# Linear attention in chunks of 64 tokens instead of 128, with all score masks on VectorE

## The reference

```python
q, k = relu(q) + 1e-6, relu(k) + 1e-6
kv = cumsum(einsum('bhld,bhle->bhlde', k, v), axis=2)
num = einsum('bhld,bhlde->bhle', q, kv)
den = maximum(einsum('bhld,bhld->bhl', q, cumsum(k, axis=2)), 1e-6)
out = (num / den) @ out_w.T + out_b
```

## Time and profile before

| | |
|---|---|
| Median of 3 runs | 380.64 us (379.93 to 380.88) |
| Span of the profiled execution | 377.9 us |
| Around the span (median less span) | 2.7 us |
| TensorE busy | 356.6 us, 94% of the span |
| VectorE busy | 296.1 us, 78% |
| GpSimd busy | 279.1 us, 74% |
| ScalarE busy | 162.6 us, 43% |

### The profile page before, as it was taken

One profiled execution on the slowest core, in us unless ns is written; L12 is line 12 of the kernel. 1 busy time (PEld: TensorE's weight loads), 2 busy tenths in 40 slices (PEclk: granted clock), 3 DMA queues, 4 the chain that ended last, 5 costly groups with the idle time before them and its releaser, 6 DMA issues. The chain is left out here.

```text
span 377.9 us, 10670 instructions
## 1 busy us (share of the span) xinstructions
PE 356.6 (94%) x3514; PEld 255.6 (68%) x3514; DVE 296.1 (78%) x922; ACT 162.6 (43%) x394; POOL 279.1 (74%) x414
## 2 busy tenths in 40 slices
PE   8999999999999999999999999999899989998781
PEld 4566677777677777767777777778676556655451
DVE  2588788898989898888898878886756588799462
ACT  2463553454455346436436524442456435331120
POOL 5338987766777866877867789898978888578455
PEclk9999999999999999999999999999999999999897
DMA  8993881200300120032121013003000233148750
GB/s 255 328 308 88 251 245 22 66 16 16 72 31 16 35 53 16 19 83 87 55 49 39 25 25 67 16 20 80 16 31 28 73 97 111 57 146 283 220 181 23
DMA packets 39309, 34.50 MB, mean 91 GB/s; under 512 B 4505, under 2 KB 38456, under 8 KB 39256
## 3 DMA queue, kind: packets, MB, share of 16 engines
q1 hardware_dynamic: 36392, 29.54, 27.7%
q0 software_dynamic: 1312, 3.37, 2.9%
q10 hardware_dynamic: 1552, 0.92, 0.9%
HBM read 17.55 MB, written 12.60 MB: 80 GB/s over the span
## 5 line engine op out<-in xcount | busy, mean ns | idle before, releaser
L1650 POOL TENSOR_TENSOR s_t<-s_t,causal 128x512 f32<-128x512 f32 x63 | 78.9, 1273 | 15.6 <-ACT s_t L961 15.4
L539 PE MATMUL bank<-h1t,w_qkv 128*128 128x512 f32 x112 | 52.9, 595 | 0.4 <-DVE x L1220 0.3
L1207 DVE TENSOR_TENSOR s_t<-sbank,causal 128x512 f32<-128x512 f32 x65 | 43.5, 671 | 1.1 <-PE sbank L560 1.0
L1642 POOL TENSOR_TENSOR state_wide<-state,own_pair 128x256 f32<-128x256 f32 x28 | 18.9, 676 | 25.5 <-DVE state L1198 24.4
L961 ACT ACTIVATE s_t<-sbank 128x512 f32<-128x512 f32 x63 | 33.7, 587 | 7.8 <-PE sbank L560 7.8
L560 PE MATMUL sbank<-arena 32*128 32x256 f32 x512 | 36.7, 400 | 0.0
L599 PE MATMUL bank<-s_t,vp 128*32 128x128 f32 x1024 | 34.6, 275 | 1.1 <-DVE s_t L1207 0.4
L546 PE MATMUL bank<-w_qkv,h1t 128*128 128x256 f32 x128 | 34.2, 389 | 0.0
L1658 POOL TENSOR_TENSOR rr<-ve,neg_half 128x3 f32<-128x3 f32 x36 | 31.9, 887 | 3.0
L684 PE MATMUL bank<-w_out,attn_t 128*128 128x256 f32 x128 | 33.6, 385 | 0.5 <-DVE attn_t L1288 0.5
L778 PE MATMUL sbank<-h1t,w 128*128 128x512 f32 x72 | 33.0, 596 | 0.5 <-ACT h1t L961 0.5
(11 more groups left out here) (231 smaller groups left out, 831.5 us busy)
## 6 DMA issues: line engine op xcount, KB each, us to landing
rden_t<-rden SPq DMA_DIRECT2D x64, 64.0 KB
rows<-x SPq DMA_DIRECT2D x32, 128.0 KB, 1.7
x<-in_x SPq DMA_DIRECT2D x7, 512.0 KB, 8.6
out<-x SPq DMA_DIRECT2D x7, 512.0 KB
we<-in_we SPq DMA_DIRECT2D x1, 2048.0 KB
xmask<-in_mask POOLq DMA_DIRECT2D x2, 616.0 KB, 10.3
rows<-empty SPq DMA_DIRECT2D x1, 1032.0 KB, 5.2
we<-in_we SPq DMA_DIRECT2D x1, 1024.0 KB
```

Source lines behind the costliest of these rows:

```text
L539: mm = pe.matmul(dst[:, :], w_qkv[:, ch, cb * P:(cb + 1) * P], h1t[:, g % 3, ch, :], start=(ch == 0), stop=(ch == CH - 1))
L1207: dve.tensor_tensor(s_t[:, r, :, :], sbank[r][:, :].rearrange("p (s q) -> p s q", s=4), causal[:, :].unsqueeze(1).to_broadcast([P, 4, P]), ...
L1650: pool.tensor_tensor(s_t[:, r, :, :], s_t[:, r, :, :], causal[:, :].unsqueeze(1).to_broadcast([P, 4, P]), ALU.mult)\
```

## The change

Scores, masks and numerators are formed in chunks of 64 tokens. The two chunks of a tile lie side by side in the partitions: chunk c has its keys in partitions 64c to 64c+63. Scores of a tile take half the columns. The state is now advanced twice per tile, `inner_state` (between the two chunks) and `next_state`, each a 128x64 sum from PSUM; the parity factor moves into `own_block`, by which GpSimd multiplies (512 elements per partition instead of 256). Numerators move from bank 3 into free columns of score banks 2 and 3, so that `scores` of a tile now waits for `attn_t` and both state sums. Score tiles `s_t` are double. All four banks of scores are masked by VectorE in two instructions (512 elements each, two banks at a time), both at the start of its step. ScalarE's copies and GpSimd's masks go. The numbers of small matmuls change: `scores` 8 to 16 per tile, `numerators` 16 to 32, `from_state` 2 to 16, `key_values` 8 to 16.

The core of the diff:

```diff
 def scores(t):
-    wait(pe, s_masked, 2 * t)
-    wait(pe, s_copied, 2 * t)
+    wait(pe, s_masked, on_dve(t))
+    wait(pe, attn_ready, t)
+    wait(pe, state_ready, states(t + 1))
...
+            for c in range(2):
+                for r in range(RG):
+                    both = sbank[r][chunk(c), 2 * ch * CK:2 * (ch + 1) * CK].rearrange("p (s n) -> p s n", s=2)
+                    mm = pe.matmul(both, kt(slot, ch)[rows, part(t, c)], qpair(slot, ch)[rows, :, part(t, c)],
+                                   start=True, stop=True)
...
 def numerators(t):
+                v_of = vp[chunk(c), t % 3, head // 2, 32 * par:32 * par + 32]
+                mm = pe.matmul(sbank[2 + c][32 * r:32 * r + 32, at:at + CK], v_of,
+                               s_t[chunk(c), t % 2, r, 2 * ch + par, :],
...
+def inner_state(t):
+    wait(dve, st_done, t + 1)
...
+        dve.tensor_tensor(now, sums_of(0), state[:, t % 3, 0, :, :].rearrange("p c e -> p (c e)"), ALU.add)\
+            .then_inc(state_ready, 1)
+def next_state(t):
+    wait(dve, state_ready, states(t) + 1)
...
+def mask_scores(t, r):
+    dve.tensor_tensor(s_t[:, t % 2, r:r + 2, :, :],
+                      sall[:, r:r + 2, 0:4 * CK].rearrange("p r (a n) -> p r a n", a=4),
+                      causal_ck[:, :].unsqueeze(1).unsqueeze(1).to_broadcast([P, 2, 4, CK]), ALU.mult)\
+        .then_inc(s_masked, 1)
...
 def step(pool, i):
+    wait(pool, state_ready, states(M) + 1)
+    wait(pool, num_done, M - 1)
+    pool.tensor_tensor(state_wide[:, M % 2, c:2, :, :, :].rearrange("p k c r e -> p (k c) r e"),
...
-    for r in range(on_act(M + 1) - on_act(M)):
-        wait(pool, s_copied, 2 * M + r + 1)
```

More of the change, by code:

```diff
@@ L349, in tok, with part, chunk @@
             return slice((t % GT) * P, (t % GT + 1) * P)
+        def part(t, c):
+            first = (t % GT) * P + c * CK
+            return slice(first, first + CK)
+        def chunk(c):
+            return slice(c * CK, (c + 1) * CK)
         def starts(t):
@@ L578, in from_state @@
                 slot = (t // GT) % 2
-                wait(pe, h1t_ready, min(t + 1 + AHEAD + 1, NT))
-                wait(pe, x2_ready, t - 2)
-                wait(pe, wide_ready, updates(t))
-                for ch in range(CH):
-                    pe.matmul(bank[3][:, ch * P:(ch + 1) * P],
-                              state_wide[:, (t - 1) % 2, ch, :, :].rearrange("p r e -> p (r e)"),
-                              qall(slot, ch)[:, tok(t)], start=(ch == 0), stop=False, skip_group_check=True)
+                wait(pe, s_copied, on_act(t + 1))
+                wait(pe, s_masked, on_dve(t + 1))
+                wait(pe, wide_ready, t + 1)
+                for c in range(1 if starts(t) else 0, 2):
+                    for ch in range(CH):
+                        for r in range(RG):
+                            at = D + ch * CK
+                            pe.matmul(sbank[2 + c][32 * r:32 * r + 32, at:at + CK], state_wide[:, t % 2, c, ch, r, :],
+                                      qall(slot, ch)[:, part(t, c)], start=(ch == 0), stop=False, skip_group_check=True)
             def numerators(t):
-                wait(pe, h1t_ready, min(t + 1 + AHEAD + 1, NT))
-                wait(pe, x2_ready, t - 2)
                 first = starts(t)
@@ L637, in step @@
                     mm.then_inc(sc_done, 1)
-                if is_tile(V):
-                    wait(pe, ktok_ready, K + 1)
-                    values(V)
-                if i > NT:
-                    gate_products(pe, i - NT - 1, 1)
-                if is_tile(M) and not starts(M):
-                    from_state(M)
                 if i == NT - 1:
@@ L651, in step @@
                 if is_tile(M):
+                    from_state(M)
                     numerators(M)
[L653 to L667 removed]
                 if i == 0:
@@ L670, in step @@
                     pe.wait_ge(prep_dve, 5)
+                if is_tile(K):
+                    key_values(K)
+                if i > NT:
+                    gate_products(pe, i - NT - 1, 1)
+                if is_tile(F):
+                    wait(pe, x2_ready, i - 3)
+                    tr_h1(F, bank[3])
+                if is_tile(V):
+                    wait(pe, ktok_ready, K + 1)
+                    values(V)
+                if is_tile(K) and K % GT == 0:
+                    denominators(K // GT)
                 if is_tile(K):
@@ L1184, in by_queries @@
                 dve.tensor_tensor(qkc(g % 2, ch), ksum(g % 2, ch), qall(g % 2, ch), ALU.mult).then_inc(qkc_ready, 1)
-            def new_state(t):
-                u = updates(t)
-                wait(dve, st_done, u + 1)
-                wait(dve, wide_ready, updates(t - 2))
-                wait(dve, state_ready, 2 * u)
-                added = bank[3][:, D:D + CH * 2 * HD].rearrange("p (c s e) -> p c s e", c=CH, s=2)
-                for par in range(2):
-                    own = parity[:, par:par + 1]
-                    now = state[:, t % 3, :, par, :]
-                    if starts(t):
-                        dve.tensor_scalar(now, added[:, :, par, :], own, None, ALU.mult).then_inc(state_ready, 1)
-                    else:
-                        dve.scalar_tensor_tensor(out=now, in0=added[:, :, par, :], scalar=own,
-                                                 in1=state[:, (t - 1) % 3, :, par, :], op0=ALU.mult, op1=ALU.add)\
-                            .then_inc(state_ready, 1)
@@ L1202, in mask_scores @@
-            def mask_scores(t, lo=0, hi=RG):
-                own = range(on_act(t + 1) - on_act(t), RG)
-                for r in own[lo:hi]:
-                    wait(dve, s_done, t + 1)
-                    wait(dve, num_done, t)
-                    dve.tensor_tensor(s_t[:, r, :, :], sbank[r][:, :].rearrange("p (s q) -> p s q", s=4),
-                                      causal[:, :].unsqueeze(1).to_broadcast([P, 4, P]), ALU.mult)\
-                        .then_inc(s_masked, 1)
+            def inner_state(t):
+                wait(dve, st_done, t + 1)
+                wait(dve, wide_ready, t - 1)
+                wait(dve, state_ready, states(t))
+                now = state[:, t % 3, 1, :, :].rearrange("p c e -> p (c e)")
+                if starts(t):
+                    dve.tensor_copy(now, sums_of(0)).then_inc(state_ready, 1)
+                else:
+                    dve.tensor_tensor(now, sums_of(0), state[:, t % 3, 0, :, :].rearrange("p c e -> p (c e)"), ALU.add)\
+                        .then_inc(state_ready, 1)
@@ L1215, in step @@
                 if is_tile(M):
-                    mask_scores(M, 0, 1 if i < NT else RG)
+                    mask_scores(M, 0)
+                    mask_scores(M, 2)
                 if is_tile(X1):
```

193 lines of the change are left out of this document (99 added, 94 removed).

## The result

Changed kernel: 420.31 us (median of 4 runs, 417.52 to 421.05), before beside it 380.76 (379.93 to 381.10): ratio 1.101, interval 1.096 to 1.106. The forecast was 399 with 379 to 414, so the time lies above the range. The side is right, the size is not: 22.4 us of the profiled span are unexplained by the forecast.

A forecast was written before the change was run, and what follows sets the result against it. TensorE set the period before; afterwards the loop through VectorE, lengthened by the SBUF port, would. 15 + 1.5 + 2 = +18.5 on a 377.9 span gives 396.4, plus 2.7 around it 399 us; own range 393 to 405, with rivals 379 to 414.

The forecast's parts named there:

- The loop through VectorE closes and TensorE's saving is gone: Main loop: x to `attn_t` 4.46 plus back 3.43 is 7.89, so TensorE's 0.56 per step is gone.
- The port: SBUF port: GpSimd's `state_wide` starts 0.06 ahead of VectorE's scan, which ends 1.08 behind it; +15 over steps 4 to 23.
- waited for only through the port, ScalarE by nobody: GpSimd's masks and ScalarE's copies go at no gain: GpSimd's loop work matters only through the port, nobody waits for ScalarE.
- The 4.46 from x to `attn_t`: First half of the loop, through `qk_block`, cross scores, `from_state`, `numerators` and keys-values sum: 4.46 us.
- the forecast's waves: TensorE's `numerators`: 64 records of 64 columns, eight tiles at once, 8 waves x 0.055 + 0.12 = 0.56.
- the DMAs that spread the reciprocals: SP's eight DMAs ahead of `attn_t`: taken at 0; if they needed all of 6.93, 10 us in all.
- Rival C: Eight tiles at once fail or small matmuls issue too slowly: +16 on top, 415 us; chance 0.12.
- Steps 28 to 31: No `qk_block`, so not this loop; TensorE's own about 5.8 per step plus 0.55 once: 23.8 us.
- Up to step 3: Steps 2 and 3 have the loop through VectorE already: +1 us each.
- A: Port conflict missed: scan starts first wherever statistics are of three tiles, steps 4 to 22 stay at 8.05: 385; chance 0.20.
- B: Loop through VectorE closes later, TensorE keeps setting the period: 365 with all 0.56 per step, 373 with half; chance 0.15.
- D: TensorE's starts have a floor, 24 ns each, that more tiles do not lift: +49, 448 us; chance 0.03.

The follow-up runs named there:

- reordered 3: Changed kernel, reordered: output product and transposed prob ahead of `scores` on TensorE, scan and both by_queries ahead of `attn_t`, exp ahead of ScalarE's copies; 384.13 us, ratio 1.008.

## Why the prediction was wrong in size

1. "The loop through VectorE closes and TensorE's saving is gone": right. TensorE waits for x ahead of `qk_block`, 16.2 us in all, and freeing the loop piece by piece takes 420 down to 384.
2. The port: right in type 1 and in steps 25 to 27, with its size, and hidden in type 2 of steps 4 to 23. `state_wide` starts 0.10 to 0.51 ahead of the scan (forecast 0.06), the scan ends 1.08 behind it, `attn_t` to x is 4.41 in type 1 (4.50), and in steps 25 to 27, where no exp is late, 4.41, 4.41 and 4.50 (4.50, 4.50, 4.56). Step 21, VectorE's timeline, then GpSimd's:

```profile
228.48 2.00 DVE L1198 TENSOR_TENSOR_SCAN arena<-arena,zero 128x512 f32<-128x512 f32 x1
228.14 1.27 POOL L1670 TENSOR_TENSOR state_wide<-state,own_block 128x512 f32<-128x512 f32 x1 [0.49 <-DVE state L1215]
```

 In type 2 the late exp kept the scan away from `state_wide`: 1.22 to 1.28 long, where 2.2 was forecast. Freeing the port gave 14.8 us once `rsum` was out of the way, the forecast's largest term being 15; that the two agree so well is in part luck, since of steps 4 to 23 the changed kernel paid for the scan's wait in the five of type 1, where the forecast had ten. The Trainium skill's rule cited there ("SBUF — State Buffer", Terms) holds by these scans, and the runs add that a tenth of a us settles who waits.
3. The step that failed first: GpSimd is "waited for only through the port, ScalarE by nobody". ScalarE is waited for, by `rsum`. The change moved the `h1` transposes behind the keys-values sum; on ScalarE their copy stands ahead of the exp; VectorE's `rsum` stands ahead of `next_state`. The forecast priced the move of the transposes on TensorE and followed it into no other queue. Measured: 5.01 and 4.96 for `attn_t` to x in types 2 and 3, where 4.50 and 4.24 or 4.56 were forecast; 8 us by the two kernels that undo it.
4. The 4.46 from x to `attn_t`: mis-sized. Undisturbed it is 4.70. TensorE's distances from first start to next start, before, forecast and after:

| | before | forecast | after |
|---|---|---|---|
| `scores` | 1.076 | 0.53 | 0.627 |
| `numerators` | 0.898 | 0.56 | 0.659 |
| `from_state` | 0.537 | 0.56 | 0.584 |
| keys-values | 0.237 | 0.22 | 0.391 |
| cross scores | 0.404 | 0.36 on the loop | 0.495 |

 Each is 0.02 to 0.17 over the forecast: 64 records of `numerators` start 0.642 apart from first to last, 10 ns each, where the forecast's waves give 7 x 0.055 = 0.39. Adding all groups of a step without waits, with the transposes and values (0.06 and 0.05 dearer), the saving is 0.29, not 0.56. On the loop it is cross scores (0.13), `numerators` (0.10) and `from_state` (0.02) that make 4.70 of 4.46; over 20 steps the 0.24 are 4.8 us.
5. Taken at nothing: the supply of instructions and the DMAs that spread the reciprocals. The mean of x to `attn_t` is 4.91, 0.21 over the undisturbed 4.70, another 4.2 us in steps 4 to 23. Three stalls of 0.34, 0.58 and 0.62 there are 1.5 of it. In four of the five steps of type 1 `attn_t` starts 0.16 to 0.63 later behind the last keys-values product than usual, 1.3 together, which fits the DMAs; no run tests it. Steps 12 and 19 have such a delay too, 0.35 and 0.37, and what holds them stays open. Rival C spoke of issue that is too slow and priced a steady pace. The pace was reached (10 ns); what it lacked is that the program itself comes in packets, and that price shows in whole stalls, 8 of them in the whole trace, 4.1 us together.
6. Steps 28 to 31: 28.8 us, forecast 23.8. "TensorE's own, from numerators over `attn_t` and state to `scores`, is about 5.8" left out the transposes and the wait for `h2t`. Before, these four steps took 26.6 of the 57.70 in the earlier trace rows, so that 23.8 forecast a gain of 2.8 that nothing had been named for.
7. Up to step 3: +6.5 instead of +2. Steps 2 and 3 show the late exp and the stalls as later ones do (`rsum` 2.15 behind `attn_t` in step 3, a stall of 0.72 in step 2).

Points 3 to 5 are the +12.9 of steps 4 to 23: 0.25, 0.24 and 0.21 of the 0.69 by which the period from x to x (9.49) lies over 8.80. Rivals A and B fell; D too, with 10 ns where it asked for 24. The Trainium skill's floor of 25 ns ("TensorE: Matmul & The Clock Gate", Wait — 56ns, not 53.3ns?) does not hold across tiles here: 64 records of `numerators` start 10 ns apart.

## What to carry to other kernels

When a producer is moved on one engine, follow each of its consumers into its own queue, and list what stands behind it there: an in-order queue turned a copy that nobody was in a hurry for into 8 us on the critical loop. Count a kernel's instructions as well as its columns: where small matmuls double TensorE's program and the engine is near its bound, their saving is partly given back in stalls (7.7 us in reordered 3), and the sign to look for is a gap with no releaser inside a group, here always 1.2 to 1.8 us behind a packet of the instruction queue. And free the loop before judging the change: nine tenths of the +39.6 us went with the order (420 to 384), and what is left, +3.6, I read as TensorE's saving less its dearer small groups and their supply. No run separates these.

## What the runs showed of the hardware that I had not expected

- By the counts above TensorE's program arrives in 16 KB packets of 256 instructions while the kernel runs, and TensorE stops in some places until 1.16 to 1.77 us after a packet's end: 123 of 123 stalls, mostly 0.3 to 0.9 us, up to 3.5. Why the delay behind a packet is that long, and what decides when a packet is asked for, these traces don't say.
- A stall of 1.2 to 3.5 us (once a halt of 1.78 between two groups) was followed in seven cases, five in one trace and two in another, by 3.4 to 6.8 us at half the granted clock: a missing instruction costs a second time. Five other stalls of 1.2 to 1.8 us were not, so length alone does not decide it.
- Small matmuls in eight tiles (two row strips by four column strips) start at 10 ns a record in a steady run of 64, so neither a floor of 24 nor the 15 ns of the earlier trace rows holds. Matmuls that move only 64 columns but have 128 columns of weights started 110 ns apart over the full array, and 27.7 in four strips.
- A wait elsewhere can hide a port conflict (step 22 of the changed kernel, `rsum` held by the exp: scan 1.22; with that wait gone: 2.26), and an added wait can be worth 15 us (411.94 to 397.10).
